# Scores and maxima written and read in pairs of PSUM banks, and the order of the steps planned in periods of two

## The reference

```
xn = layernorm(x)                                   # over 256 features
q, k, v = split(xn @ w_qkv + b_qkv)
scores = q @ k.T * 0.25;  scores[j < i] = -inf      # each token sees itself and later ones
s = (softmax(scores) @ v) @ w_out + b_out
h = s0 * (concat(xn, -xn) @ sign(k0)); h = relu(h) * 2   # 512 -> 1024
h = s1 * (h @ sign(k1));               h = relu(h) * 2   # 1024 -> 1024
g = silu(s2 * (h @ sign(k2)))                            # 1024 -> 256
out = x + s * g
```

## Time and profile before

| | |
|---|---|
| median of 3 runs | 2552.58 us (2552.55 to 2552.8) |
| the profiled execution | 2555.14 us |
| its span, first to last instruction | 2553.4 us |
| PE, DVE, ACT, POOL busy | 2455.9, 1823.4, 1542.0, 913.5 us |
| first maxima, first scores, last scores begin | 177.8, 234.3, 2519.2 us |
| mean granted TensorE clock | 0.98 |

### The profile page before, as it was taken

One profiled execution on the slowest core, in us unless ns is written; L12 is line 12 of the kernel. 1 busy time (PEld: TensorE's weight loads), 2 busy tenths in 40 slices (PEclk: granted clock), 3 DMA queues, 4 the chain that ended last, 5 costly groups with the idle time before them and its releaser, 6 DMA issues.

```text
span 2553.4 us, 50994 instructions
## 1 busy us (share of the span) xinstructions
PE 2455.9 (96%) x17616; PEld 1478.7 (58%) x17616; DVE 1823.4 (71%) x4516; ACT 1542.0 (60%) x3135; POOL 913.5 (36%) x1080
## 2 busy tenths in 40 slices
PE   7989999999999999999999999999999999999986
PEld 6877555555555555555555555555555555555552
DVE  7767867677777777777777777777767777777712
ACT  5652656666666666666666665666666665666642
POOL 1014223332433434243433433343434434343532
PEclk9998999999999999999999999999999999999986
DMA  8981111011111212131212212121212122121321
GB/s 317 356 328 45 39 29 53 21 53 29 52 35 40 74 47 69 41 86 34 77 43 69 58 35 79 44 78 41 78 36 81 42 55 67 43 73 42 95 88 47
DMA packets 157805, 192.67 MB, mean 75 GB/s; under 512 B 65276, under 2 KB 102076, under 8 KB 157560
## 3 DMA queue, kind: packets, MB, share of 16 engines
q1 hardware_dynamic: 156600, 189.41, 24.4%
q10 hardware_dynamic: 960, 0.00, 0.0%
HBM read 112.13 MB, written 76.14 MB: 74 GB/s over the span
## 4 chain that ended last, share of the span: by engine, by line
PE 86%; DMA 4%; DVE 3%; ACT 2%; POOL 2%; issue 2%; SPq 1%; POOLq 0%; ACTq 0%; DVEq 0%
PE b_ps L1083 21%; PE b_pv_ps L1061 21%; PE b_ps L1029 18%; PE b_ps L1041 11%; PE b_ps L1080 5%; PE b_ps L1087 5%; PE b_ps L1106 3%; DMA a_xs<-L_attn_x 2%; ACT b_probs L1141 1%; PE a_qk_ps L290 1%; DMA b_xs<-L_attn_x 1%; DVE a_stats L396 1%; DVE a_qk_parts L434 1%; DVE b_part_max L1196 1%; PE b_ps L1049 1%
## 5 line engine op out<-in xcount | busy, mean ns | idle before, releaser
L1141 ACT ACTIVATE b_probs<-b_ps 128x512 f32<-128x512 f32 (+3 forms) x2560 | 1216.9, 534 | 687.2 <-PE b_ps L1029 684.8
L1196 DVE TENSOR_REDUCE b_part_max<-b_ps 128x1 f32<-128x512 f32 x1536 | 976.9, 682 | 296.3 <-PE b_ps L1041 295.0
L1193 DVE CUSTOM_DVE_ANT_0 b_ps<-b_ps,k_mask 128x512 f32<-128x512 f32 (+3 forms) x1024 | 483.2, 515 | 255.0 <-PE b_ps L1041 251.6
L1061 PE MATMUL b_pv_ps<-b_probs,k_vst 128*32 128x512 f32 (+3 forms) x5120 | 604.6, 544 | 12.7 <-issue 8.6
L1029 PE MATMUL b_ps<-k_qst,k_kst 50*128 50x512 f32 (+3 forms) x2560 | 594.2, 461 | 6.2 <-DMA k_qst<-b_max_parts 3.2
L1029 PEld LDWEIGHTS b_ps<-k_qst,k_kst 50*128 50x128 f32 x2560 | 239.9, 184 | 548.7 <-DVE b_part_max L1196 193.0
L1083 PE MATMUL b_ps<-b_u_hi,k_w 128*128 128x256 f32 x2048 | 534.3, 296 | 3.9 <-POOL b_u_lo L965 3.8
L1041 PE MATMUL b_ps<-k_kst,k_qst 48*128 48x512 f32 (+3 forms) x2560 | 493.4, 379 | 28.3 <-ACT b_probs L1141 20.7
L1083 PE MATMUL b_ps<-b_u_lo,k_w 128*128 128x256 f32 x2048 | 519.9, 289 | 0.0
L1083 PEld LDWEIGHTS b_ps<-b_u_hi,k_w 128*128 128x128 f32 x2048 | 392.6, 192 | 62.9 <-issue 47.4
L963 POOL CAST b_u_hi<-b_u 128x512 fp32r<-128x512 f32 x256 | 156.1, 610 | 753.4 <-ACT b_u L1169 753.2
(11 more groups left out here) (101 smaller groups left out, 1849.9 us busy)
## 6 DMA issues: line engine op xcount, KB each, us to landing
qk_parts<-a_qk_parts SPq DMA_DIRECT2D x64, 512.0 KB, 3.8
k_kst<-qk_parts SPq DMA_DIRECT2D x384, 64.0 KB, 2.3
k_qst<-qk_parts SPq DMA_DIRECT2D x384, 64.0 KB, 2.3
a_xs<-L_attn_x SPq DMA_DIRECT2D x16, 512.0 KB, 5.6
xn_T<-a_xT SPq DMA_DIRECT2D x16, 512.0 KB, 5.1
v_plain<-a_v_out SPq DMA_DIRECT2D x16, 512.0 KB, 5.0
k_xf<-xn_T SPq DMA_DIRECT2D x32, 256.0 KB, 3.3
b_v_in<-v_plain SPq DMA_DIRECT2D x64, 128.0 KB, 2.6
```

The lines of the kernel that those rows point to most:

```text
L1061: mm = pe.matmul(pv_ps[h * VW:(h + 1) * VW, 0:cols], vst[:, kb // TT, kb % TT, h, :], probs[:, s % P_SLOTS, h, 0:cols], start=start, stop= ...
L1141: act.activation(probs[:, s % P_SLOTS, h, 0:cols], ps[:, banks[place, half][0], 0:cols], ACT.Exp, scale=HD ** -0.5).then_inc(exp_done, 1)
L1193: dve.tensor_tensor_reduce(src, src, mask[:, 0:CHUNK - k0 % CHUNK], 1.0, -3.0e38, ALU.add, ALU.max, dst).then_inc(ring_read, 1)
L1196: dve.tensor_reduce(dst, src, AX_X, ALU.max).then_inc(ring_read, 1)
```

## The change

- **Pairs.** `ps` is now three pairs of banks; F has one bank of its own, `f_ps`. S and M write both banks of a pair, and one semaphore increment stands on the second matmul. ACT takes one exp over both banks (128x1024), DVE one reduce with two results; on the diagonal DVE still runs two masked reduces, with one increment. negmax, project and the like take a whole pair and use its first bank. `banks_of` deals the pairs out strictly in turn.
- **Periods of two steps.** Events of steps t and t+1 (t even) are placed together. The four S stand at 1.0, 1.2, 3.1 and 5.1, four M at 1.1, 3.0, 3.2 and 5.0 (in catching up a fifth at 5.2, a sixth at 0.9), F at 2.0 and 4.5, the PV of step t-2 at 4.0 and that of step t-1 at 6.0. A full period reads S M S, F, M S M, PV, F, M S, PV. In the lead F stands at 2.0, 4.0, 4.5 and 6.0.
- **Others.** The mask of the even step comes at 2.5, of the odd one at 0.5 of the next period; `keep` stands one step behind, at 0.0; negmax at 1.9, behind S M S; both halves of project at 1.8 of an even step. recip, scale and bias keep their steps; those of odd steps now come behind all of the period.

```diff
-PV_LAG, M_LEAD = 2, 21
+M_LEAD = 21
-BANKS = 7
+BANK_PAIRS = 3
+SCORE_PLACES = ((1.0, 1.2), (3.1, 5.1))
+MAX_PLACES = {4: (1.1, 3.0, 3.2, 5.0), 5: (1.1, 3.0, 3.2, 5.0, 5.2), 6: (0.9, 1.1, 3.0, 3.2, 5.0, 5.2)}
+VALUE_PLACES = ((2, 4.0), (1, 6.0))
+NETWORK_PLACES = (2.0, 4.5)
...
             t = base + s
+            period = t - t % 2
             for pair in range(PAIRS):
-                out.append((t, 2.0 * pair, "S", n, s, pair))
+                out.append((period, SCORE_PLACES[t % 2][pair], "S", n, s, pair))
             if kb < TT * (c + 1):
-                out.append((t + 1, 0.5, "mask", n, s))
-            out.append((t + PV_LAG, 3.0, "PV", n, s))
+                out.append((even(t), 0.5 if t % 2 else 2.5, "mask", n, s))
+            behind, place = VALUE_PLACES[t % 2]
+            out.append((t + behind, place, "PV", n, s))
...
-                out += [(t, 2.5, "neg", n, c), (t + 2, 1.0, "negmax", n, c)]
+                out += [(t, place + 0.05, "neg", n, c), (t + 2, 1.9, "negmax", n, c)]
...
-    places = [(t, p) for t in range(-LEAD, 0) for p in (1.1, 3.05)]
-    places += [(t, 1.1) for t in range(GROUPS * STEPS - 6)]
+    places = [(t, p) for t in range(-LEAD, 0, 2) for p in (2.0, 4.0, 4.5, 6.0)]
+    places += [(t, p) for t in range(0, GROUPS * STEPS - 6, 2) for p in NETWORK_PLACES]
...
-                out += [(t + gap + half, 1.0 + 0.001 * n, what, e, i, half) for half in range(2)]
+                out += [(even(t + gap) if what == "project" else t + gap + half, 1.8 + 0.001 * n, what, e, i, half)
+                        for half in range(2)]
...
+    counts = {"exp": 0, "ring": 0}
+    for at, (what, *_) in enumerate(order):
+        kind = {"S": "exp", "M": "ring", "negmax": "ring", "fold_bias": "ring", "project": "ring", "last_sums": "ring",
+                "last_project": "ring"}.get(what)
+        if kind:
+            pair = len(out) % BANK_PAIRS
+            counts[kind] += 1
+            out[at] = (pair, *last.get(pair, (None, 0)))
+            last[pair] = (kind, counts[kind])
...
-        ps = pb("ps", [P, BANKS, CHUNK])
+        ps = pb("ps", [P, BANK_PAIRS, HALVES, CHUNK])
+        f_ps = pb("f_ps", [P, FPU, PIECE])
...
-                    outs = [claimed((place, half)) for half in range(HALVES)]
+                    dst = claimed(place)
...
-                        pe.matmul(outs[half][:, 0:cols], keys, qst[rows, c, pair, 0:cols],
-                                  start=True, stop=True).then_inc(s_ready, 1)
+                        mm = pe.matmul(dst[:, half, 0:cols], keys, qst[rows, c, pair, 0:cols], start=True, stop=True)
+                    mm.then_inc(s_ready, 1)
...
                     if lo == 0:
-                        claimed(("F", use))
+                        if use > 0:
+
+                            pe.wait_ge(f_read, use)
...
+                    act.wait_ge(s_ready, g * SCORES + s * PAIRS + pair + 1)
+                    act.activation(probs[:, s % P_SLOTS, heads, 0:cols], ps[:, banks[place][0], :, 0:cols], ACT.Exp,
+                                   scale=HD ** -0.5).then_inc(exp_done, 1)
...
+                    else:
+                        dve.tensor_reduce(part_max[ib // TT % 2][:, row::PAIRS * TT, kc], src[:, :, 0:cols], AX_X, ALU.max
+                                          ).then_inc(ring_read, 1)
```

More of the change, by code:

```diff
@@ L540, in attention_events @@
     out = []
+    in_period = {}
+    for n in range(GROUPS):
+        for u in range(len(units)):
+            t = max_step(n * STEPS + u // PAIRS)
+            in_period.setdefault(t - t % 2, []).append((n, u))
+    place_of = {}
+    for t, those in in_period.items():
+        for place, (n, u) in zip(MAX_PLACES[max(4, len(those))], those):
+            place_of[n, u] = (t, place)
     for n in range(GROUPS):
@@ L651, in banks_of @@
     last = {}
[L652 to L656, removed]
-                        "F": ("f", 1)}.get(what, (None, 0))
-        for k in range(number):
-            use = ("F", arg[0]) if what == "F" else (at, k)
-            if use not in out:
-                bank = free.pop(0)
-                counts[kind] += 1
-                out[use] = (bank, *last.get(bank, (None, 0)))
-                last[bank] = (kind, counts[kind])
-            if what != "F" or arg[8]:
-                free.append(out[use][0])
+    counts = {"exp": 0, "ring": 0}
[7 more added lines that the diff above has]
+            last[pair] = (kind, counts[kind])
     return out
@@ L1007, in claimed @@
             def claimed(use):
-                bank, reader, count = banks[use]
+                pair, reader, count = banks[use]
                 if reader == "exp":
@@ L1013, in claimed @@
                     pe.wait_ge(ring_read, count)
-                elif reader == "f":
-                    pe.wait_ge(f_read, count)
-                return ps[:, bank]
+                return ps[:, pair]
             for place, (what, *arg) in enumerate(order):
@@ L1037, in _ @@
                         pe.wait_ge(k_loaded[kc], (g + 1) * HALVES * PARTS * DMA)
-                    outs = [claimed((place, j))[:, 0:CHUNK - k1] for j in range(HALVES)]
+                    dst = claimed(place)
                     for j in range(HALVES):
                         rows = slice(j * HALF, j * HALF + DEPTH)
-                        pe.matmul(outs[j], qst[rows, c, pair, i * P:(i + 1) * P],
-                                  kst[rows, k_slot(kc, g % 2), pair, k1:CHUNK], start=True, stop=True
-                                  ).then_inc(ring_ready, 1)
+                        mm = pe.matmul(dst[:, j, 0:CHUNK - k1], qst[rows, c, pair, i * P:(i + 1) * P],
+                                       kst[rows, k_slot(kc, g % 2), pair, k1:CHUNK], start=True, stop=True)
+                    mm.then_inc(ring_ready, 1)
                 elif what == "negmax":
                     g, c = arg
-                    dst = claimed((place, 0))
+                    dst = claimed(place)[:, 0]
                     pe.wait_ge(padded, 1)
@@ L1132, in _ @@
                     cols = steps[s][2]
[L1133 to L1142 removed]
+                    heads = slice(pair * HALVES, (pair + 1) * HALVES)
+                    if pair == 0 and g * STEPS + s == 0:
+                        act.wait_ge(kept.stored, 1)
+                    if pair == 0 and g * STEPS + s >= P_SLOTS:
+                        act.wait_ge(pv_done, g * STEPS + s - P_SLOTS + 1)
+                    act.wait_ge(s_ready, g * SCORES + s * PAIRS + pair + 1)
+                    act.activation(probs[:, s % P_SLOTS, heads, 0:cols], ps[:, banks[place][0], :, 0:cols], ACT.Exp,
+                                   scale=HD ** -0.5).then_inc(exp_done, 1)
                 elif what == "out":
@@ L1168, in _ @@
                         layer = 0 if kind == "L0" else 1
[L1169 removed]
+                        act.activation(u[:, split % U_SLOTS], f_ps[:], ACT.Relu,
                                        scale=kept.sign[:, layer:layer + 1]).then_inc(f_read, 1)
@@ L1241, in _ @@
                 elif what == "last_sums":
-                    src = ps[:, banks[place, 0][0]]
+                    src = ps[:, banks[place][0], 0]
                     for half in range(2):
```

84 lines of the change are left out of this document (35 added, 49 removed).

## The result

The changed kernel takes **2631.96 us** (median of 4 runs, 2627.62 to 2635.61) against 2552.69 for the kernel before (2552.55 to 2553.11): 1.0295 times as long, 95% interval 1.0273 to 1.0317. It is 79 us, 3%, **slower**. The prediction had 2544.5 us and a range of 2500 to 2580: the sign is wrong, and the time lies above the range.

What follows compares the result with a forecast made beforehand. The prediction took PE's own pace (96% busy) as the bound; -58 us for fewer stretches and smaller terms, mostly waits, summed to -8, from 2555.1 to 2547 profiled, so 2544.5 us as median; range 2500 to 2580.

Steps and rivals of the forecast that it cites:

- The 58 us of fewer stretches: On PE: T stretches fall from 1258 to 961, F stretches from 623 to 614, saving 58 us.
- Rival 3: A further unit in a T stretch costs 0.34 us, its weights waiting for the same rows: +31, 2576 us; chance 0.03.
- PV to F as PV to S: On PE: PV straight to F, new and 291 times, costs the same full price as PV to S.
- Rival 1: PV to F is free on PE, since both use all 128 rows: 58 us less, 2486; chance 0.07.
- the recurrence of one full period: PE's claims against reader ends over two steps: 7.43 us, no stall, the last three claims with 0.1 to 0.3 us slack.
- Rival 2: The M at 7.77 waits for its pair's reduce from about 1.26 us on: 2590 us, at half 2567; chance 0.22.
- The transposes: The transpose of the maxima behind S M S waits 0.75 us for the first S's exp, 62 times: +46 us.
- project: Two in a row behind S M S in 13 cases, the first waiting 0.75 us: +10 us.
- F's claim: F's weight load no longer waits for exps, 81 waits at 0.1 us each: -8 us, ends 0 and -22.
- The bursts left by an empty F place: Periods with an F place left empty: PE's waits cost 45 us before and 34 after, net -11 us.
- the L2 pieces: Two activations of 0.69 us ahead of the last exp in half of 32 cases, 0.3 us each: +5 us.
- Rival 4: The transpose's wait is partly no loss, letting ACT and DVE catch up: -33 us, 2512; chance 0.20.

Runs made afterwards that it cites:

- half_reduce: The changed kernel with the unmasked reduces reading only half of the columns, leaving out half of the maxima; 2583.38 us, 1.0112 of the kernel before.
- network_last: The changed kernel with the second F of a period moved from 4.5 to 5.5, between last M and PV; 2592.86 us, 1.0141 of the kernel before.
- behind_f_single: Seven single banks, transpose and project at 5.6 behind the second F, late F places empty only before a PV of 512; 2522.28 us, 0.9876 of before.

## Why the prediction was wrong, point by point

- **The 58 us of fewer stretches: right** (57 by the split, 53 to 60 with other prices). So were its prices: S to M 0.34, M to S 0.24 (1104.05 to 1104.29), the last of a stretch of three 0.33. Rival 3, a further unit at 0.34, is out. So, for this case, is the sentence of the Trainium skill that it came from (TensorE: Matmul & The Clock Gate, Part 3, Packing small matmuls, that weight loads overlap matmuls in flight only in another row group); the same section also lets a load go ahead into a background weight buffer, which the prediction left out, and the 0.24 fits that.
- **PV to F as PV to S: right.** PV costs 1.00 us before F (1107.02 to 1108.02) and 0.99 before S (1110.18 to 1111.17). Rival 1 is out: the column-tiled PV shares all rows with F, and the change of kind costs all the same.
- **The readers: right.** The reduce took 1.22 us, as predicted. The exp of 1024 columns took 1.02 (1.03 predicted).
- **The step that failed: the recurrence of one full period, which ends in "No stall".** It was worked for a period whose PVs are 512 wide, and gave a slack of 0.1 us for the head M (there at 7.77, needed 7.6). I had put 512, 128, 384 and 256 into the description of a step, and 0.36 us for a PV of 128 was to be had from the same prices. In the 128 heads behind a short PV the slack is not 0.1 but -0.67 and -0.34. With the exposed weight load that is 73 us, 83 with the heads of 384 columns, in a place whose price in the sum was zero. The clock, 23 us by the estimate above, had no term either.
- **Rival 2 had the place and missed the point.** It named this very M, and this reduce as what it waits for, but made it hang on the reduce's length (1.26 us and more) in all of some 290 periods. The reduce was shorter than that. What decided was how long PE takes to come back.
- **The transposes: 22 us for 46; project: right,** 10 for 10 (S to the first project 1.07 us instead of some 0.3 in 11 cases and 1.28 in one; the two at the very end wait for their input as before). The size of one wait was right (1.08 for 0.34 us), the number was not: where the head M waits, the transpose doesn't. half_reduce and network_last, where the head M is in time or nearly, have 38 and 46.
- **F's claim: 14 us gained for 8**, M to F lost 7.0 us instead of 21.5. F to F lost 23 instead of 14. Of these 9 us, 4 are the lead, where four F stretches wait 1.0 us each for the read of the single bank (the +4 of the prediction); nearly all the rest are matmuls at half clock, 0.21 us apart and not 0.12.
- **The small terms.** Masked reduces: 7 us for 6. The end: from the last S on 34 us before and after, so 0 for -2. The bursts left by an empty F place (-11) and the L2 pieces (+5) I have not told apart in the traces.
- **Rival 4, waits that are partly no loss,** holds only in that waits stand in for each other, the head M for the transpose. It came out as two waits of which one is paid, not as one that costs nothing.
- **The size of the range.** Its upper end, 2580, was cut from rival 2 as I had priced it. The claim with the least slack got one price, for one width.

## What to carry to other kernels

When an order is planned by hand around rotating buffers, work the slack of each claim (time between the two claims of a buffer, less the time until its reader is done) for every shape that stands between them, shortest first; the steady case tells the most only if it is the tightest. In this kernel three pairs in turn wanted the longest non-claiming work (F) between the last user and the next, and the extra claims directly behind such work; seven single banks wanted much the same (behind_f_single). A removed wait shows the one beside it, so moves are worth trying together: two of them gave -42 and +6 us alone, -82 together with the empty places chosen, and -124 with the claims moved once more and the empty places chosen by width.

## What the runs showed of the hardware

- A row-tiled unit that waited makes the next one about 0.08 us late: after, M to S is 0.31 us and not 0.23 behind a head M that waited. In 249 places M to S is more than 0.05 us over its price (21 before). In 189 of them it is over by 0.05 to 0.11, which makes 14 us in all; in the others the S waits itself, or the clock is low. The trace shows whence the 0.08 come: the weight loads of an M that needn't wait start 0.11 us ahead of it, those of the M at 1311.44 only 0.03 ahead.

```profile
1297.34 0.21 PEld L1050 LDWEIGHTS b_ps<-k_kst,k_qst 48*128 48x128 f32 x2
1297.45 0.41 PE L1050 MATMUL b_ps<-k_kst,k_qst 48*128 48x512 f32 x2
...
1311.41 0.21 PEld L1050 LDWEIGHTS b_ps<-k_kst,k_qst 48*128 48x128 f32 x2 [0.80 <-issue]
```

- The granted clock can fall to its lower level in the middle of a stretch in which PE is 90% busy: to a mean of 0.52 from 1575 to 1589 us, behind 14 us with PE busy 12.68. There a 256-column matmul takes 0.21 us instead of 0.12.
- One instruction over two PSUM banks is little cheaper than two. The reduce takes 1.22 us for 1.29, the exp 1.02 for 0.48 + 0.60 = 1.08. Advanced Engine Details and Errata of the Trainium skill (TRN2 Errata, The Read-Write Bubble) lists it as a way around a bubble between instructions; the trace agrees in kind, and shows how small it is at 512 columns a bank: 0.06 to 0.07 us of 1.1 to 1.3, while the first bank comes free 0.4 to 0.5 us later (1.02 for 0.60, 1.22 for 0.68).
